# Four cross-attention layers on one core: two scaled tiles of a narrow layer added into one, entries in one plan with a new list

## The chip, the cores and the metric
One core of one Trainium2 chip runs the whole program. The metric is the device time in microseconds, as the median of runs. Engines: PE (TensorE), DVE (VectorE), ACT (ScalarE), POOL (GpSimd) and SP (SyncE, which only issues DMAs here).

## The reference
The stream x has 4 batches of 1024 tokens with 256 channels, the context 4 x 154 x 512. Layers 0 and 2 are wide (16 heads of 64, a mask on two pairs of keys), layers 1 and 3 narrow (RMS norm first, 16 heads of 16 that share 4 key-value groups). All add to the stream.

```python
# wide                                   # narrow
q, k, v = x @ Wq, ctx @ Wk, ctx @ Wv     # xn = x * rsqrt(mean(x*x) + eps) * norm_w
logits = q.k * 64**-0.5 + col_bias       # q, k, v = xn @ wq, ctx @ wk, ctx @ wv
out = softmax(logits) @ v                # out = softmax(q.k * 16**-0.5) @ v   (k, v: 4 groups)
x = x + out @ Wo + bo                    # x = x + out @ wo
```

## The kernel before
The program has three parts: prepare (weights split into a high and a low float32 part, keys and values of all layers made and stored in DRAM), run_layers, and store_outputs. The change is in run_layers, with small edits in prepare.

**Tiles.** Work is done transposed, channels on partitions and 512 tokens along the free axis. A batch is two token halves; a wide and a narrow layer on both halves make four chunks: 0 wide half 0, 1 narrow half 1 (of the batch before), 2 wide half 1, 3 narrow half 0. Each chunk has four steps, so a window has 16 steps, four heads each. There are 8 windows (4 batches, 2 pairs of layers), and the ones at either end are only partly filled.

**A step.** The list ORDER is a text of entries; every engine walks it in the same order and does its own part of each entry. query makes q on PE (L1271), ACT and DVE split it into q_pair and q_aux (L1033 to L1034, L1170 to L1173). max is a bf16 product of one (narrow) or two (wide) passes (L1290, L1286) into one of three PSUM banks called general, reduced by DVE to row maxima (L1183). turn transposes the maxima. rest and score are the products (L1314 to L1317, L1325 to L1326) into two banks, ACT takes the exponential (L1046). value multiplies by v into out_ps (L1341 to L1367), and ACT copies to the buffer kept (L1068), 12 tiles of 128 x 512.

**After a chunk.** sums: SP stores the softmax sums to DRAM and loads them spread over the partitions. inverse: DVE takes reciprocals (L1190), SP stores them (L934) and broadcasts those of the first pair of tiles into inv_b (L906, spread_inverses: 2 DMAs if wide, 4 if narrow). scale n k: POOL multiplies two tiles of kept by inv_b (L1143), then SP broadcasts the next pair. norm: ACT copies both tiles to a_hi (L1082). low: DVE makes a_lo = kept - a_hi (L1196). output: PE multiplies by the output weights (L1384) for both halves of the channels, tile by tile, with three passes for a split product (hi hi, hi lo, lo hi), and DVE adds to x (L1216). A wide chunk has four such batches of two tiles, a narrow chunk two: OUT_BATCHES = (4, 2, 4, 2).

**Narrow tiles.** A narrow tile holds one key-value group's four heads in four blocks of 32 partitions. In each block 16 rows are the head's output and the other 16 hold the sum, since the value matrix has 16 columns of v and 16 of ones; the weights no have zeros in the rows of the sums. Two groups that follow each other have their blocks exchanged in pairs (block_of).

**Keys and weights.** nkeys n (four parts, 13 DMAs each, 14 in the first) and wkeys n load the next keys through SP's queue (L847, L815), in the places that the list gives them. At window 4 the second pair of layers begins: SP also loads the other query, output and narrow weights (L769, L792, L805), behind the entries that free them.

**Order around the change.** An entry with "-" belongs to the window before, with "+" to the one after. The bank of a use of general is its number among such uses in the list modulo 3, and bank() (L1239) makes PE wait for the reader of the use three before that is present. Engines are in order: whatever an entry waits for holds everything behind it on that engine.

## Time and profile before

| | us |
|---|---|
| median of 3 runs | 1891.38 (1888.63 to 1896.26) |
| profiled execution | 1886.37 |
| its span | 1883.9 |
| PE busy | 1703.7 (90%) |
| DVE busy | 1251.6 (66%) |
| ACT busy | 1040.1 (55%) |
| POOL busy | 428.8 (23%) |

A name such as general<-a_hi,wo_hi says what an instruction writes and reads. PE's passes overlap: one is shown as busy until its last row is out, though the next has begun. In brackets behind a row of a timeline stands the engine's idle time before it and what ended it.

### The profile page before, as it was taken

The numbers are of one execution on the slowest core, as the hardware profiler recorded it, in microseconds if no ns is written. First come the engines' busy times: TensorE is split into PE (matmuls) and PEld (weight loads), VectorE is DVE, ScalarE is ACT, GpSimd is POOL, SyncE is SP. The second block draws the span as 40 slices with busy tenths as digits, with TensorE's granted clock in tenths as the row PEclk, the third lists the DMA queues.
The fourth block names the chain that finished last, engine by engine and source line by source line (L and its number), as shares of the span: only waits on it lengthen the run. The fifth ranks groups of instructions, "written<-read, shape, count | busy, mean of one in ns | idle before, by whom it ended". The sixth has DMA issues, their size and how long they took to land. (4 is left out here: it accounts for less than half of the span.)

```text
span 1883.9 us, 29965 instructions
## 1 busy us (share of the span) xinstructions
PE 1703.7 (90%) x10924; PEld 935.7 (50%) x10924; DVE 1251.6 (66%) x2393; ACT 1040.1 (55%) x1761; POOL 428.8 (23%) x299
## 2 busy tenths in 40 slices
PE   6897597989999999999899999899999999999574
PEld 5786333444545454545445454445454545454333
DVE  4447554667867786878566777577777777776342
ACT  1111063666666666666566666566666666666231
POOL 4242302121222122212111322121212121312201
PEclk9998698999999999999999999999999999999786
DMA  8976542051215121513243324222332233221205
GB/s 270 326 266 207 130 125 47 13 102 35 75 44 124 35 75 44 124 36 95 69 100 76 88 49 101 58 70 60 83 65 71 60 82 66 70 60 50 56 25 201
DMA packets 176025, 175.78 MB, mean 93 GB/s; under 512 B 89538, under 2 KB 131902, under 8 KB 174281
## 3 DMA queue, kind: packets, MB, share of 16 engines
q1 hardware_dynamic: 173576, 163.39, 33.0%
q10 hardware_dynamic: 2304, 10.49, 1.4%
q8 instruction: 88, 1.44, 0.3%
q14 instruction: 57, 0.46, 0.1%
HBM read 127.17 MB, written 46.63 MB: 92 GB/s over the span
## 5 line engine op out<-in xcount | busy, mean ns | idle before, releaser
L1183 DVE TENSOR_REDUCE tops<-general 128x2 bf16<-128x308 f32 x1024 | 436.6, 472 | 105.3 <-PE general L1290 47.8
L1143 POOL TENSOR_TENSOR kept<-kept,inv_b 128x512 f32<-128x512 f32 x192 | 258.6, 1368 | 659.6 <-DMA inv_b<-scratch_inverses 655.3
L1046 ACT ACTIVATE probs<-score_ps 128x512 f32<-128x512 f32 x512 | 299.4, 597 | 137.9 <-PE score_ps L1326 130.4
L1170 DVE CAST q_aux<-q_pair 64x512 bf16<-64x512 f32 x160 | 82.7, 517 | 211.4 <-ACT q_pair L1034 210.3
L1056 ACT ACTIVATE q_aux<-general 4x512 bf16<-4x512 bf16 x320 | 187.6, 586 | 13.6 <-PE general L1297 6.7
L1033 ACT ACTIVATE q_pair<-general 64x512 fp32r<-64x512 f32 x160 | 94.6, 592 | 178.3 <-PE general L1271 178.0
L1082 ACT ACTIVATE a_hi<-kept 128x512 fp32r<-128x512 f32 x192 | 109.9, 621 | 122.3 <-POOL kept L1143 62.8
L1196 DVE TENSOR_TENSOR a_lo<-kept,a_hi 128x512 fp32r<-128x512 f32 x192 | 149.8, 821 | 28.6 <-ACT a_hi L1082 27.8
L1216 DVE TENSOR_TENSOR x<-general,x 128x512 f32<-128x512 f32 x160 | 108.4, 690 | 80.5 <-PE general L1384 79.2
L1286 PE MATMUL general<-w_top,q_aux 128*128 128x154 bf16 x1024 | 125.7, 234 | 24.0 <-DVE q_pair L1173 10.5
L1131 POOL TENSOR_TENSOR x_lo<-xn,x_hi 128x1024 fp32r<-128x1024 f32 x32 | 75.8, 2368 | 308.0 <-ACT x_hi L1014 157.1
L1341 PE MATMUL out_ps<-probs,w_val 128*64 128x512 f32 x512 | 136.5, 617 | 0.7 <-ACT probs L1046 0.7
L1290 PE MATMUL general<-n_top,q_aux 128*128 128x308 bf16 x512 | 129.5, 301 | 6.7 <-DVE q_aux L1171 2.9
L1068 ACT ACTIVATE kept<-out_ps 128x512 f32<-128x512 f32 x192 | 104.2, 595 | 56.5 <-PE sum_ps L1355 41.5
L1325 PE MATMUL score_ps<-q_pair,n_pair 128*128 128x512 f32 x256 | 124.3, 494 | 8.6 <-ACT probs L1046 7.1
L1271 PE MATMUL general<-x_hi,wq_hi 128*128 128x512 f32 x256 | 114.8, 449 | 19.0 <-POOL x_lo L1131 18.6
L1286 PEld LDWEIGHTS general<-w_top,q_aux 128*128 128x128 bf16 x1024 | 79.0, 99 | 103.2 <-issue 38.0
L1384 PE MATMUL general<-a_hi,wo_hi 128*128 128x512 f32 x256 | 112.4, 439 | 14.8 <-DVE q_pair L1173 6.6
L1325 PE MATMUL score_ps<-q_pair,w_pair 128*128 128x512 f32 x256 | 122.1, 481 | 0.8
L1172 DVE TENSOR_TENSOR q_pair<-general,q_pair 64x512 fp32r<-64x512 f32 x160 | 109.5, 684 | 5.0
L1173 DVE TENSOR_TENSOR q_pair<-general,q_pair 64x512 fp32r<-64x512 f32 x160 | 111.0, 694 | 2.2
L1046 ACT ACTIVATE probs_rest<-score_ps 128x512 f32<-128x512 f32 x128 | 76.3, 596 | 56.7 <-PE score_ps L1326 38.6
(150 smaller groups left out, 3249.3 us busy)
## 6 DMA issues: line engine op xcount, KB each, us to landing
inv_b<-scratch_inverses SPq DMA_DIRECT2D x128, 256.0 KB
inv_b<-scratch_inverses SPq DMA_DIRECT2D x128, 128.0 KB
xn<-scratch_stream SPq DMA_DIRECT2D x16, 512.0 KB, 3.8
w_pair<-scratch_wk_hi SPq DMA_DIRECT2D x32, 256.0 KB
x<-scratch_stream SPq DMA_DIRECT2D x16, 512.0 KB, 3.3
scratch_stream<-x SPq DMA_DIRECT2D x16, 512.0 KB, 4.0
scratch_wk_hi<-p_kout_hi SPq DMA_DIRECT2D x16, 308.0 KB
p_raw<-in_L_xattn_Wk_dram SPq DMA_DIRECT2D x4, 1024.0 KB, 6.9
```

The source lines that it names most:

```text
L1046: nc.scalar.activation(dst, score_ps[:, number % 2, :], ACT.Exp, scale=scale).then_inc(act_exp.sem, 1)
L1056: last = nc.scalar.activation(q_aux[a:a + 4, half_of(n), slot(n), j, :], ps[0:4].bitcast(BF16)[:, 0:TOK], ACT.Copy, scale=-1.0)
L1143: last = nc.gpsimd.tensor_tensor(tile, tile, inv_b[:, i, :], ALU.mult)
L1173: last = nc.vector.tensor_tensor(q_pair[0:64, s, j + 1, :], ps[64:P], q_pair[64:P, s, j + 1, :], ALU.subtract)
L1183: last = nc.vector.tensor_reduce(tops[:, n % 2, sub, 2 * pair:2 * pair + 2], src, AX_X, ALU.max)
L1196: last = nc.vector.tensor_tensor(a_lo[:, i, :], kept[:, place(tile), :], a_hi[:, i, :], ALU.subtract)
L1271: last = nc.tensor.matmul(ps, l, r, start=(i == 0), stop=(i == len(pairs) - 1))
L1286: last = nc.tensor.matmul(ps[:, i * KEYS:(i + 1) * KEYS], q[:, 2 * pair + i, sub], w_top[:, 4 * (n % 4) + 2 * pair + i, :], start=True, st ...
L1290: last = nc.tensor.matmul(ps[:, 0:2 * KEYS], q[:, n % 2, sub], n_top[:, h:h + 2, :].rearrange("p h k -> p (h k)"), start=True, stop=True)
L1325: nc.tensor.matmul(ps, keys[0], q_pair[:, s, unit, :], start=True, stop=False)
L1341: last = nc.tensor.matmul(out_ps[64 * i:64 * i + 64, k, :], w_val[:, h * DW:(h + 1) * DW], probs[:, 2 * k + i, :], start=True, stop=False, ...
L1384: last = nc.tensor.matmul(ps, l, r, start=(i == 0), stop=(i == len(pairs) - 1))
```

## The change
In a narrow batch, the inverses are spread into a buffer of their own, inv_n, which is zero in the rows of the other group's place, so that scaling also clears the rows of the sums. For this, prepare puts v of every second group in the other 16 columns of a block. POOL then adds the second tile to the first (with a wait for its own product). norm, low and output handle that one tile, and the weights no hold both groups in one tile of 128 rows. The inverses in DRAM are doubled, one for wide and one for narrow chunks; an inverse therefore waits for the chunk two before. The rows of the sums are stored with two DMAs. inv_n takes 8 DMAs of 16 rows each, where 4 of 32 rows and two tiles were.

Beside that, the entries of all windows are written out once into one PLAN, with those left out that don't exist. Banks of general and score_ps follow from the number in this plan. ORDER is a new list with the same entries in another order (one max entry, one norm and one low are in the window beside).

```diff
-        sums=d("sums", (H, TOK), F32), inverses=d("inverses", (H, TOK), F32),
+        sums=d("sums", (H, TOK), F32), inverses=d("inverses", (2, H, TOK), F32),
...
-                    last = nc.vector.tensor_copy(nvout[0:m, n % OUTS, :, 0:DN], ps[0:m, bank, 0:KVN * DN].rearrange("p (g d) -> p g d", g=KVN))
+                    src = ps[0:m, bank, 0:KVN * DN].rearrange("p (v g d) -> p v g d", g=2, d=DN)
+                    dst = nvout[0:m, n % OUTS].rearrange("p (v g) d -> p v g d", g=2)
+                    for g in range(2):
+                        last = nc.vector.tensor_copy(dst[:, :, g, g * DN:g * DN + DN], src[:, :, g, :])
...
-            nc.gpsimd.memset(nvout[:], 0.0).then_inc(s_pool, 1)
-            pool.wait_ge(s_pool, 2)
-            for u in range(KVN):
-                nc.gpsimd.memset(nvout[:, :, u, DN:], 1.0)
+            nc.gpsimd.memset(nvout[:], 1.0)
...
 ORDER = """
...
-    rest 8, output 0 1, score 8 0, max 9 0, max 9 1, score 8 1, max 9 2, score 8 2, max 9 3, norm 0 2,
-        max 9 4, value 8 0, max 9 5, nkeys 0 0, max 9 6, max 9 7, score 8 3, scale 0 3, low 0 2, sums 1,
-        query 10 0, turn 9, inverse 1, value 8 1, output 0 2, max 10 0, norm 0 3, low 0 3, nkeys 0 1,
-    rest 9, max 10 1, max 10 2, query 10 1, score 9 0, score 9 1, output 0 3, squares 3, score 9 2,
-        max 10 3, score 9 3, max 10 4, value 9 0, max 10 5, max 10 6, square 3, max 10 7, query 11 0,
-        query 11 1, turn 10, value 9 1, rate 3, max 11 0, max 11 1,
-    rest 10, max 11 2, score 10 0, max 11 3, nkeys 0 2, max 11 4, max 11 5, score 10 1, nkeys 0 3,
-        max 11 6, max 11 7, score 10 2, score 10 3, query 12 0, turn 11, scale 1 0, early 0+, value 10 0,
-        value 10 1, max 12 0, max 12 1, max 12 2,
...
-    rest 13, max 14 7, score 13 0, max 15 0, max 15 1, score 13 1, max 15 2, score 13 2, turn 14,
-        score 13 3, low 1 1, wkeys 0+ 1, max 15 3, query 0+ 0, scale 2 0,
-    rest 14, output 1 1, norm 2 0, value 13 1, max 15 4, max 15 5, score 14 0, max 15 6, scale 2 1,
-        score 14 1, max 15 7, max 0+ 0, max 0+ 1, score 14 2, max 0+ 2, low 2 0, score 14 3, max 0+ 3,
-        turn 15, query 0+ 1,
-    rest 15, value 14 1, score 15 0, output 2 0, wkeys 0+ 2, score 15 1, max 0+ 4, wkeys 0+ 3, score 15 2,
-        norm 2 1, max 0+ 5, max 0+ 6, score 15 3, max 0+ 7, low 2 1, query 1+ 0, turn 0+, value 15 1,
-        scale 2 2, output 2 1, norm 2 2, scale 2 3, max 1+ 0, low 2 2, query 1+ 1
...
+    rest 1, score 1 0, output 2- 3, score 1 1, max 2 1, squares 1, score 1 2, max 2 2, max 2 3, value 1 0,
+        max 2 4, max 2 5, square 1, sums 3-, score 1 3, max 2 6, max 2 7, query 3 0, query 3 1, turn 2,
+        value 1 1, rate 1, max 3 0,
+    rest 2, inverse 3-, max 3 1, max 3 2, max 3 3, early 2, score 2 0, max 3 4, score 2 1, scale 3- 0,
+        max 3 5, max 3 6, score 2 2, max 3 7, score 2 3, query 4 0, turn 3, value 2 0, value 2 1, max 4 0,
+        max 4 1, max 4 2,
+    rest 3, max 4 3, max 4 4, max 4 5, score 3 0, max 4 6, score 3 1, max 4 7, max 5 0, norm 3- 0,
+        score 3 2, max 5 1, score 3 3, low 3- 0, max 5 2, query 6 0, turn 4, scale 3- 1, value 3 0,
+        max 5 3, value 3 1, max 5 4, sums 0, max 5 5, max 5 6,
...
+    rest 8, low 0 1, max 9 2, max 9 3, query 9 1, score 8 0, sums 1, score 8 1, output 0 1, norm 0 2,
+        value 8 0, max 9 4, score 8 2, max 9 5, max 9 6, score 8 3, max 9 7, nkeys 0 0, low 0 2,
+        query 10 0, nkeys 0 1, turn 9, nkeys 0 2, value 8 1, output 0 2, max 10 0, norm 0 3, low 0 3,
+        query 10 1,
+    rest 9, score 9 0, output 0 3, score 9 1, max 10 1, max 10 2, squares 3, score 9 2, nkeys 0 3,
+        max 10 3, value 9 0, max 10 4, max 10 5, square 3, score 9 3, max 10 6, max 10 7, query 11 0,
+        query 11 1, turn 10, value 9 1, rate 3, inverse 1, max 11 0, max 11 1,
+    rest 10, max 11 2, max 11 3, score 10 0, max 11 4, score 10 1, max 11 5, max 11 6, score 10 2,
+        max 11 7, score 10 3, query 12 0, value 10 0, turn 11, scale 1 0, value 10 1, max 12 0, max 12 1,
+        max 12 2,
+    rest 11, max 12 3, score 11 0, max 12 4, max 12 5, score 11 1, max 12 6, max 12 7, score 11 2,
+        max 13 0, score 11 3, max 13 1, max 13 2, norm 1 0, value 11 0, max 13 3, early 0+, low 1 0,
+        max 13 4, query 14 0, turn 12, value 11 1, max 13 5, sums 2, scale 1 1,
+    rest 12, wkeys 0+ 0, max 13 6, max 13 7, max 14 0, score 12 0, output 1 0, turn 13, score 12 1,
+        max 14 1, score 12 2, max 14 2, max 14 3, max 14 4, score 12 3, norm 1 1, max 14 5, max 14 6,
+    rest 13, inverse 2, value 12 1, low 1 1, split 0+, max 14 7, score 13 0, max 15 0, max 15 1,
+        score 13 1, output 1 1, scale 2 0, wkeys 0+ 1, turn 14, score 13 2, score 13 3, max 15 2, max 15 3,
+        query 0+ 0, wkeys 0+ 2,
+    rest 14, value 13 1, max 15 4, max 15 5, wkeys 0+ 3, score 14 0, score 14 1, norm 2 0, max 15 6,
+        scale 2 1, max 15 7, scale 2 2, max 0+ 0, score 14 2, max 0+ 1, turn 15, low 2 0, score 14 3,
+        scale 2 3, max 0+ 2, query 0+ 1,
+    rest 15, output 2 0, value 14 1, score 15 0, max 0+ 3, score 15 1, max 0+ 4, max 0+ 5, norm 2 1,
+        score 15 2, score 15 3, max 0+ 6, max 0+ 7, low 2 1, query 1+ 0, turn 0+, query 1+ 1, value 15 1,
+        output 2 1
 """
...
+def plan():
+
+    entries = []
+    for r in range(-1, ITER + 1):
+        entries += [(r + turn, what, n, k) for what, n, k, turn in WINDOW if present(r + turn, what, n)]
+    return entries
+
+
+PLAN = plan()
...
-GENERAL = [(*x, m) for x in WINDOW if x[0] in ("query", "max", "turn", "output", "square", "rate")
-           for m in range(KC if x[0] == "output" else 1)]
-assert len(GENERAL) % GB == 0
-BANK = {(*use[:3], use[4]): i % GB for i, use in enumerate(GENERAL)}
+GENERAL = [(*x, m) for x in PLAN if x[1] in ("query", "max", "turn", "output", "square", "rate")
+           for m in range(KC if x[1] == "output" else 1)]
+USE = {use: i for i, use in enumerate(GENERAL)}
...
-        no = [sb(f"no_{a}", [P, KVN, C], F32R) for a in ("hi", "lo")]
+        no = [sb(f"no_{a}", [P, KVN // 2, C], F32R) for a in ("hi", "lo")]
...
-        inv_b = sb("inv_b", [P, 2, TOK])
+        inv_b, inv_n = sb("inv_b", [P, 2, TOK]), sb("inv_n", [P, 2, TOK])
...
-        sums_stored, sums_loaded = signal("sums_stored", "sums", times=16), signal("sums_loaded", "sums", times=16)
-        inv_stored, inv_loaded = signal("inv_stored", "inverse", times=16), signal("inv_loaded", "scale", times=64)
+        sums_stored, sums_loaded = signal("sums_stored", "sums", times=32), signal("sums_loaded", "sums", times=16)
+        inv_stored = signal("inv_stored", "inverse", times=16)
+        inv_loaded = [Signal(sem("wide_inv_loaded"), ("scale",), 32, (0, 2)), Signal(sem("narrow_inv_loaded"), ("scale",), 16 * 8, (1, 3))]
...
+        pool_parts = Signal(sem("pool_parts"), ("scale",), only=(1, 3))
...
-                            at = 32 * block_of(v, j)
-                            dst = no[i][at:at + DN].rearrange("p (k v) n -> p k v n", v=2)
-                            sp.dma_start(dst[:, :, v, :].bitcast(F32), src[v, j]).then_inc(narrow_out_loaded, 16)
+                            at = 32 * block_of(v, j) + DN * v
+                            sp.dma_start(no[i][at:at + DN].bitcast(F32), src[v, j]).then_inc(narrow_out_loaded, 16)
...
             def spread_inverses(c, batch):
 
-                for h in range(2 if c % 2 == 0 else 4):
+                rows = dr["inverses"][c % 2]
+                for h in range(2):
                     if c % 2 == 0:
                         dst = inv_b[64 * h:64 * h + 64, :, :]
-                        src = dr["inverses"].rearrange("(h i g) n -> g h i n", h=2, i=2)[batch:batch + 1, 1 - h]
+                        src = rows.rearrange("(h i g) n -> g h i n", h=2, i=2)[batch:batch + 1, 1 - h]
+                        sp.dma_start(dst, src.to_broadcast([64, 2, TOK])).then_inc(inv_loaded[0].sem, 16)
                     else:
-                        dst = inv_b[32 * h:32 * h + 32, :, :]
-                        src = dr["inverses"].rearrange("(j g) n -> j g n", g=4)[h:h + 1, 2 * batch:2 * batch + 2]
-                    sp.dma_start(dst, src.to_broadcast([dst.shape[0], 2, TOK])).then_inc(inv_loaded.sem, 32 if c % 2 == 0 else 16)
-
-            def one_round(r):
-
-                for what, c, k, turn in WINDOW:
-                    w = r + turn
-                    if not present(w, what, c):
-                        continue
+                        for j in range(4):
+                            at = 32 * j + DN * h
+                            src = rows[4 * j + 2 * batch + h:4 * j + 2 * batch + h + 1]
+                            sp.dma_start(inv_n[at:at + DN, h, :], src.to_broadcast([DN, TOK])).then_inc(inv_loaded[1].sem, 16)
...
-                            sp.dma_start(dr["sums"], wide_sums[0:P:8]).then_inc(sums_stored.sem, 16)
+                            sp.dma_start(dr["sums"], wide_sums[0:P:8]).then_inc(sums_stored.sem, 32)
                         else:
                             wait(sp, act_keep.sem, act_keep.after(w, "value", 4 * c + 3, 1))
                             at = place(chunk_tile(c, 0))
-                            sp.dma_start(dr["sums"].rearrange("(j g) n -> j g n", g=4),
-                                         kept[DN:P:32, at:at + 4, :]).then_inc(sums_stored.sem, 16)
+                            for v in range(2):
+                                sp.dma_start(dr["sums"].rearrange("(j g v) n -> j g v n", g=2, v=2)[:, :, v, :],
+                                             kept[DN * (1 - v):P:32, at + v:at + 4:2, :]).then_inc(sums_stored.sem, 16)
                         before_w, before = back_chunk(w, c)
                         wait(sp, dve_invert.sem, dve_invert.after(before_w, "inverse", before, 0))
                         wait(sp, sums_stored.sem, sums_stored.after(w, what, c, 0))
...
                     elif what == "inverse":
 
                         wait(sp, dve_invert.sem, dve_invert.after(w, what, c, 0))
-                        before_w, before = back_chunk(w, c)
+                        before_w, before = (w, c - 2) if c > 1 else (w - 1, c + 2)
                         wait(sp, pool_scale.sem, pool_scale.after(before_w, "scale", before, OUT_BATCHES[before] - 1))
-                        sp.dma_start(by_part(dr["inverses"]), inv[:]).then_inc(inv_stored.sem, 16)
+                        sp.dma_start(by_part(dr["inverses"][c % 2]), inv[:]).then_inc(inv_stored.sem, 16)
...
-                    for i in range(2):
+                    for i in range(1 + (n + 1) % 2):
                         tile = chunk_tile(n, 2 * k + i)
                         last = nc.scalar.activation(a_hi[:, i, :], kept[:, place(tile), :], ACT.Copy)
                     last.then_inc(act_norm.sem, 1)
...
-                    wait(pool, inv_loaded.sem, inv_loaded.after(it, what, n, k))
+                    wait(pool, inv_loaded[n % 2].sem, inv_loaded[n % 2].after(it, what, n, k))
                     wait(pool, act_keep.sem, act_keep.after(it, *tile_key(chunk_tile(n, 2 * k + 1))))
+                    tiles = [kept[:, place(chunk_tile(n, 2 * k + i)), :] for i in range(2)]
                     for i in range(2):
-                        tile = kept[:, place(chunk_tile(n, 2 * k + i)), :]
-                        last = nc.gpsimd.tensor_tensor(tile, tile, inv_b[:, i, :], ALU.mult)
+                        last = nc.gpsimd.tensor_tensor(tiles[i], tiles[i], (inv_b, inv_n)[n % 2][:, i, :], ALU.mult)
+                    if n % 2:
+                        last.then_inc(pool_parts.sem, 1)
+                        wait(pool, pool_parts.sem, pool_parts.after(it, "scale", n, k))
+                        last = nc.gpsimd.tensor_tensor(tiles[0], tiles[0], tiles[1], ALU.add)
                     last.then_inc(pool_scale.sem, 1)
 
...
                     wait(dve, act_norm.sem, act_norm.after(it, "norm", n, k))
-                    for i in range(2):
+                    for i in range(1 + (n + 1) % 2):
                         tile = chunk_tile(n, 2 * k + i)
                         last = nc.vector.tensor_tensor(a_lo[:, i, :], kept[:, place(tile), :], a_hi[:, i, :], ALU.subtract)
                     last.then_inc(dve_low.sem, 1)
...
-            def bank(it, use):
-
-                at = [(*g[:3], g[4]) for g in GENERAL].index(use)
-                turn, back = GENERAL[at][3], at - GB
-                while True:
-                    what, n, k, of, m = GENERAL[back % len(GENERAL)]
-                    w = it - turn + of + back // len(GENERAL)
-                    if present(w, what, n):
-                        break
-                    if back < -3 * len(GENERAL):
-                        return general[:, BANK[use], :]
-                    back -= GB
-                read = reader[what]
-                wait(pe, read.sem, read.after(w, what, n, k) - (read.times - 1 - m if what == "output" else 0))
-                return general[:, BANK[use], :]
+            def bank(use):
+
+                if USE[use] >= GB:
+                    w, what, n, k, m = GENERAL[USE[use] - GB]
+                    read = reader[what]
+                    wait(pe, read.sem, read.after(w, what, n, k) - (read.times - 1 - m if what == "output" else 0))
+                return general[:, USE[use] % GB, :]
...
-                        pairs = [q for i in range(2) for q in split3(w[0][:, 2 * k + i, rows], w[1][:, 2 * k + i, rows], a_hi[:, i, :], a_lo[:, i, :])]
+                        tiles = [(2 * k + i, i) for i in range(2)] if n % 2 == 0 else [(k, 0)]
+                        pairs = [q for at, i in tiles for q in split3(w[0][:, at, rows], w[1][:, at, rows], a_hi[:, i, :], a_lo[:, i, :])]
```

## Rows read from the trace of the kernel before

**Rows 1.** Page, head and part 1: busy us (share), instructions, of each engine.
```profile
span 1883.9 us, 29965 instructions
...
PE 1703.7 (90%) x10924; PEld 935.7 (50%) x10924; DVE 1251.6 (66%) x2393; ACT 1040.1 (55%) x1761; POOL 428.8 (23%) x299
```

**Rows 2.** Windows: length, busy (count) of each engine, clock, DMA share, GB/s.
```profile
core 0: us, PE busy (x) PEld busy (x) DVE busy (x) ACT busy (x) POOL busy (x), PEclk, DMA share, GB/s
...
1141.80:1339.00 197.20, 187.00 (x1250) 95.97 (x1248) 139.12 (x266) 125.39 (x216) 42.98 (x30) 0.98 0.29 69
1339.00:1527.40 188.40, 186.06 (x1250) 95.74 (x1248) 141.00 (x266) 125.55 (x217) 43.98 (x30) 1.00 0.31 70
```

**Rows 3.** Timeline of ACT: start, length, what; the x_hi splits of the same step.
```profile
1339.04 1.06 ACT L1014 ACTIVATE x_hi<-xn 128x1024 fp32r<-128x1024 f32 x1
...
1527.42 1.06 ACT L1014 ACTIVATE x_hi<-xn 128x1024 fp32r<-128x1024 f32 x1
```

**Rows 4.** Groups of PE by line and shape: busy, mean ns, idle before.
```profile
L1384 PE MATMUL general<-a_hi,no_hi 128*128 128x512 f32 x128 | 56.7, 443 | 20.7 <-DVE a_lo L1196 19.4 <-DVE q_pair L1173 1.3
```

**Rows 5.** Timeline of PE: output passes in a row.
```profile
471.54 0.40 PE L1384 MATMUL general<-a_lo,no_hi 128*128 128x512 f32 x1
...
473.87 0.39 PE L1384 MATMUL general<-a_hi,no_lo 128*128 128x512 f32 x1
```

**Rows 6.** Timeline of PE: four short bf16 passes, then a float32 one.
```profile
924.66 0.43 PE L1286 MATMUL general<-w_top,q_aux 128*128 128x154 bf16 x4
924.89 0.47 PE L1325 MATMUL score_ps<-q_pair,w_pair 128*128 128x512 f32 x1
925.21 0.39 PE L1326 MATMUL score_ps<-q_aux,w_aux 128*128 128x512 bf16 x1
```

**Rows 7.** Timeline of PE: what follows the large holes; idle time in brackets.
```profile
932.65 0.79 PE L1271 MATMUL general<-x_hi,nq_hi 128*128 128x512 f32 x1 [6.42 <-DMA n_val_rest<-scratch_nv_rest]
...
975.66 0.49 PE L1325 MATMUL score_ps<-q_pair,n_pair 128*128 128x512 f32 x1 [3.52 <-ACT probs L1046]
...
1192.92 1.94 PE L1314 MATMUL score_ps<-q_pair,w_rest 128*32 128x512 f32 x8 [9.19 <-issue]
```

**Rows 8.** Timeline of SP, the DMA queue: start, length, what is issued.
```profile
917.93 0.60 SPq L847 DMA_DIRECT2D n_pair<-scratch_nk_hi  x1
...
930.79 0.40 SPq L847 DMA_DIRECT2D n_val_rest<-scratch_nv_rest  x1
931.23 1.73 SPq L906 DMA_DIRECT2D inv_b<-scratch_inverses  x4
...
1169.22 5.05 SPq L805 DMA_DIRECT2D no_hi<-scratch_no_hi  x8
1174.31 5.52 SPq L805 DMA_DIRECT2D no_lo<-scratch_no_lo  x8
...
1190.25 1.30 SPq L906 DMA_DIRECT2D inv_b<-scratch_inverses  x2
```

**Rows 9.** Waits: engine, line, for whom; us in total, times, longest.
```profile
ACT a_hi L1082 <- POOL kept L1143: 62.8, 14, 12.8
```

**Rows 10.** Timeline of the tail: SP, POOL, PE.
```profile
1833.35 8.44 SPq L906 DMA_DIRECT2D inv_b<-scratch_inverses  x8
...
1837.59 2.48 POOL L1143 TENSOR_TENSOR kept<-kept,inv_b 128x512 f32<-128x512 f32 x2 [45.74 <-DMA inv_b<-scratch_inverses]
...
1842.63 0.79 PE L1384 MATMUL general<-a_hi,no_hi 128*128 128x512 f32 x1 [16.48 <-DVE a_lo L1196]
...
1847.49 0.53 PE L1384 MATMUL general<-a_hi,no_lo 128*128 128x512 f32 x1
```

**Rows 11.** Page, part 5, three groups; last, a line: ns min/median/max.
```profile
L1143 POOL TENSOR_TENSOR kept<-kept,inv_b 128x512 f32<-128x512 f32 x192 | 258.6, 1368 | 659.6 <-DMA inv_b<-scratch_inverses 655.3
...
L1082 ACT ACTIVATE a_hi<-kept 128x512 fp32r<-128x512 f32 x192 | 109.9, 621 | 122.3 <-POOL kept L1143 62.8
...
L1196 DVE TENSOR_TENSOR a_lo<-kept,a_hi 128x512 fp32r<-128x512 f32 x192 | 149.8, 821 | 28.6 <-ACT a_hi L1082 27.8
...
L1170 DVE CAST q_aux<-q_pair x160: 408/420/1502, 222.3 to 1796.3; 64x512 bf16<-64x512 f32 x160
```

110 lines of the change are left out of this document (46 added, 64 removed).

## The prediction
> **What bounds the kernel now.** I read first the page's part on each engine: PE is busy for 1703.7 of 1883.9 us, DVE for 1251.6 [rows 1]. That is an average over stages, so the next view is one period of the schedule. Its length is the distance between two x_hi splits of the same step: 1339.04 to 1527.42, 188.4 us [rows 3]. In that window PE is busy for 186.06 us at full granted clock, DVE for 141.00, ACT for 125.55, POOL for 43.98 [rows 2]: PE leaves 2.3 us free, the next engine 47. The window before it has the same work and is 8.8 us longer [rows 2]; its hole comes below. A busy PE may still be slow, since a pass is shown longer than it holds the engine, so I look at starts: eleven output passes in a row start between 471.54 and 473.87, ten distances in 2.33 us, though each is shown 0.39 to 0.40 long [rows 5]. I call these 0.233 us a slot. Slots stand back to back in the steady windows; what is taken off PE there is taken off the window, as long as the producers keep up. Third, PE's large holes, places that only the order decides: 6.42 us before 932.65, waiting for narrow keys, 3.52 us for ACT before 975.66, 9.19 us before 1192.92 [rows 7].
>
> **Passes removed.** A narrow batch made 2 output halves x 2 tiles x 3 split products = 12 passes, now 2 x 1 x 3 = 6. There are 16 narrow half layers of two batches each, so 32 x 6 = 192 passes go, half of three groups of 128 (one is shown) [rows 4]. At 0.233 us: 44.7 us. The most it can be is the group's shown mean, 0.443 us, 85 us [rows 4], which counts the overlap of passes twice, so I stay with the slot; the least is what the producers let through, rival B. A pass itself stays as it is: the same 512 columns, the same 128 rows, of which all now carry data.
>
> **Work moved to and from the others.** ACT loses 32 copies to a_hi of 0.621 us, 19.9 us, and DVE 32 subtractions to a_lo of 0.821 us, 26.3 us [rows 11]. Neither bounds a window, so both count as nothing there: PE's stream covers them. In the tail, where that cover is gone, they are counted. POOL gains 32 additions, priced by its products of the same form, 1.37 us, 43.8 us in all [rows 11]. With 44 of 188 us in use it has room [rows 2]. The addition also waits for the second product; no row shows such a wait, and I take 0.1 us (none to 1 us).
>
> **The SP queue.** A narrow batch issues 8 broadcasts where it issued 4, and 4 took 1.73 us [rows 8]: 1.7 us more. With POOL's addition a narrow batch is ready 3.1 us later. Behind these issues stand the early load and the next batch's spread. The chain: 4.24 us from the first issue to POOL's start (1833.35 to 1837.59) [rows 10], + 1.7, then 2 x 1.37 less overlap (shown 2.48) + 1.37 + 0.1; the store of the inverses before it I bound by what is left of the 4.24 after its issues, 2.5 us. Together 12.4 us from the reciprocal to an added tile. A step is 188.4 / 16 = 11.8 us. In the new list norm 3- 0 stands about 1.6 steps, 19 us, behind inverse 3-, and norm 1 0 as far behind inverse 1. So some 6 us of room are left, and ACT does not wait. The new wait of an inverse, for the chunk two before instead of one, is weaker than the old one: nothing.
>
> **POOL against DVE.** A cast to q_aux takes 0.408 us at least, 0.420 in the middle and 1.502 at most [rows 11]; I take the longest to lie beside POOL's work. If each of the 32 additions met one, DVE would lose 32 x 1.08 = 35 us; if none, nothing. POOL works in under a quarter of a window and DVE has 47 us of room: I take 1 us. The Trainium skill (SBUF — State Buffer, Who interferes with whom) says that GpSimd locks out, for its whole instruction, a DVE copy in a two-port mode or a DVE instruction with two SBUF inputs. By that rule, the spread of the cast's times agrees.
>
> **The new list.** (a) A float32 pass behind short bf16 ones isn't ready in time: four wide max passes from 924.66, the score pass at 924.89, the next at 925.21 [rows 6], 0.32 us instead of a slot, 0.09 more (part of it, down to none, may be given back by the last max). The new list has 42 switches from a wide max to such a pass, the old 36: 6 x 0.09 x 8 = +4.1 us. (b) The hole before 932.65. SP issued the last two key parts from 917.93 to 930.79 [rows 8], 6.5 us each, one step behind their entries. In the new list inverse 1 stands behind all four parts, and the first three follow each other without a wait from the end of step 7: 26 us, over before step 10's query 12 with some 10 us to spare: -6.4 us. (c) The hole before 1192.92. SP issued 16 pieces of the narrow output weights in 10.6 us (1169.22 to 1179.83), then an inverse's spread and two parts of the wide keys until 1190.25 [rows 8]. The 16 pieces remain; output 1 1 stands 0.6 steps earlier (-7 us), but three parts instead of two are behind it (+4.6): -2 us. (d) The hole before 975.66 is an inverse that came late behind rows of keys; now the rows go first: -1.5 us (0 to -3.5). (e) Whether the new list opens small gaps of its own, the old trace can't show. The nearest row is PE's idle time in a window, 2.3 us [rows 2]; I take no difference, and 2 us a window either way, 16 in all, for the range.
>
> **Both ends.** Preparation makes 8 more DVE copies of 64 columns; the nearest row, 0.821 us for 512 [rows 11], bounds them at 6.6 us, and I take 1. In the tail each step waits for the one before. The sums take one issue more, +0.5; the first batch comes 3.1 later for spread and addition, 0.6 and 0.7 earlier for ACT's and DVE's second tile; POOL's second start is 1.7 + 1.4 later again. But the old second batch had waited until twelve passes were over, at 0.44 us each (1842.63 to 1847.49 for eleven) [rows 10]; now there are six, and six more after. Followed through, DVE's last addition ends 2 us later than before: +2 us.
>
> **Sum.** -44.7 + 4.1 - 6.4 - 2 - 1.5 + 1 + 1 + 2 = -46.5 us. The profiled execution took 1886.37 us (2.5 us outside its span): 1839.9. It lies 5.0 us below the median of 1891.38, which is what will be compared: 1844.9 us.
>
> **Rivals.**
> A. As above, PE's slots bound every window: 1844.9, own range 1827 to 1861 from (e). 0.72.
> B. DVE sets the pace locally: the max passes use three banks that DVE empties, and the output passes were the time in which it caught up. Then only what DVE itself lost counts, 26.3 instead of 44.7 us: 1863. For it: DVE is busy for 141 of 188 us. Against: PE is idle for 2.3 us of a window. 0.10.
> C. Slower. The 6 us of room between inverse and norm aren't there, because SP still issues keys; then each of the 32 narrow batches holds ACT, in whose queue the exponentials stand behind the norm, for the chain's 3.1 us, 99 us: 1944. It decides where the chain of 12.4 us is longer than the list's distance. For it: ACT has waited for POOL 14 times, 62.8 us in all [rows 9]. Against: the distances counted above. 0.06.
> D. POOL's additions meet a cast each time, and each cast stands ahead of max passes: +34: 1879. 0.04.
> E. The list closes small gaps too, 2 us a window: 1829 or below. 0.08.
> That no passes are removed is excluded by the loops.
>
> **How the numbers follow.** The prediction is A's, 1844.9. A, B and E's larger part make up the range of 1825 to 1869; C, D and the lower part of E are left out. A measurement of this kernel can tell about 0.5%, 9.5 us, from no change. Faster by more: A, B, D and E, less 0.05 for mishaps that add up: 0.89. Within: 0.04. Slower: C and 0.01 of those: 0.07.
>
> **What would show it.** Right: 192 passes on the narrow output weights; a window of 182 to 184 us with PE idle for as little; no hole before query 12 in the fourth window, one of 5 to 9 us at the wide rest of the sixth; the tail 2 us longer. Wrong: a window of 185 to 188 us with PE waiting for tops (B), a_hi waiting for POOL in each narrow batch (C), casts with a mean far above 0.52 us (D), new holes before outputs or values (e).

## Result and the profile after

The changed kernel took 1842.7 us (median of four runs, 1835.02 to 1844.97), the kernel before 1890.14 us beside it. The ratio is 0.9738, with a 95% interval of 0.9717 to 0.9759: 49 us, or 2.6%, faster. The prediction was 1844.9 us. The profiled execution took 1840.65 us, where the sum had ended at 1839.9.

The head and first part of the page of the changed kernel, to be read beside [rows 1]:

```profile
span 1838.9 us, 29698 instructions
...
PE 1658.9 (90%) x10732; PEld 898.9 (49%) x10732; DVE 1226.8 (67%) x2370; ACT 1023.5 (56%) x1729; POOL 462.2 (25%) x327
```

PE has exactly 192 instructions fewer (10924 before), ACT 32 fewer, POOL 28 more (32 additions, and fewer of other kinds). PE's busy time fell by 44.8 us, the span by 45.0, and PE's share stayed at 90%. The three groups of output passes on the narrow weights count 64 each instead of 128 [rows 4]. The kernels differ in length, so the same line of the program has another number in each (the narrow output passes stand at L1384 before, at L1389 in the change, at L1385 to L1390 in the kernels below). Groups of PE, POOL and ACT, columns as there:

```profile
L1389 PE MATMUL general<-a_hi,no_hi 128*128 128x512 f32 x64 | 31.9, 498 | 23.8 <-DVE a_lo L1208 23.8
...
L1155 POOL TENSOR_TENSOR kept<-kept 128x512 f32<-128x512 f32 x32 | 41.5, 1298 | 2.5
...
L1090 ACT ACTIVATE a_hi<-kept 128x512 fp32r<-128x512 f32 x160 | 93.6, 624 | 103.1 <-PE general L1389 41.3 <-POOL kept L1151 33.4 <-POOL kept L1155 28.2
```

The mean of a shown pass rose from 443 to 498 ns although a pass is what it was. Half of this group's passes are the first of an output entry now, a quarter before, and a first pass is shown longer (0.50 us and more, where the others have 0.39 to 0.40). That is one more reason to count starts and not shown durations.

Two periods of the schedule, cut at the same x_hi split as [rows 2, 3]; the columns are those of [rows 2]:

```profile
1120.50:1308.80 188.30, 181.44 (x1232) 91.33 (x1224) 136.75 (x263) 123.47 (x213) 47.63 (x34) 0.99 0.30 66
1308.80:1493.40 184.60, 180.15 (x1232) 91.02 (x1224) 139.87 (x263) 123.54 (x213) 48.80 (x34) 1.00 0.30 66
```

The undisturbed period went from 188.40 to 184.60 us, the one with the hole from 197.20 to 188.30. But PE's idle time in the undisturbed one rose, from 2.3 to 4.5 us. Some of PE's waits on DVE in the whole kernel (engine, line, for whom; us in total, times, longest):

```profile
PE general L1290 <- DVE q_pair L1185: 16.9, 23, 2.2
PE general L1294 <- DVE q_pair L1185: 16.5, 13, 4.0
PE general L1294 <- DVE tops L1195: 2.4, 13, 0.2
```

L1290 and L1294 are the wide and the narrow max passes. They wait for a general bank from which DVE still reads a query (the subtraction, L1185). Before the change, PE waited for that subtraction 20.8 us in all, now 35.0 (a third line, before output passes, has 1.6).

All periods, from the same split, which readers can repeat from a timeline of ACT (us; the change is the mean of three profiled executions, whose spans are 1838.9, 1841.3 and 1840.3):

```
period               1      2      3      4      5      6   last   from last split to end
before           188.9  188.4  197.8  192.9  197.3  188.4  249.1  107.4
change           183.4  187.7  187.3  185.5  187.7  185.2  236.2  108.9
```

The stretch ahead of the first of them grew from 373.7 to 378.3 us, because the new list puts this split later; the last period gives that back, so the two belong together. The second period stands out: it moved by only 0.7 us, the first and the sixth by 5.5 and 3.2.

### The profile page after: what moved, and what is told of

It is laid out like the page before. It is cut to its first block and busy times, and to the rows that moved or that the text cites. A ratio compares the mean times of both kernels' runs of the same rounds, so it can differ in the third digit from the quotient of the medians.

```text
span 1838.9 us, 29698 instructions
## 1 busy us (share of the span) xinstructions
PE 1658.9 (90%) x10732; PEld 898.9 (49%) x10732; DVE 1226.8 (67%) x2370; ACT 1023.5 (56%) x1729; POOL 462.2 (25%) x327
## 5 line engine op out<-in xcount | busy, mean ns | idle before, releaser
L1151 POOL TENSOR_TENSOR kept<-kept,inv_b 128x512 f32<-128x512 f32 x128 | 167.0, 1326 | 427.3 <-DMA inv_b<-scratch_inverses 427.3
L1290 PE MATMUL general<-w_top,q_aux 128*128 128x154 bf16 x1024 | 130.9, 234 | 27.7 <-DVE q_pair L1185 16.9
L1090 ACT ACTIVATE a_hi<-kept 128x512 fp32r<-128x512 f32 x160 | 93.6, 624 | 103.1 <-PE general L1389 41.3
L1208 DVE TENSOR_TENSOR a_lo<-kept,a_hi 128x512 fp32r<-128x512 f32 x160 | 121.7, 793 | 39.4 <-ACT a_hi L1090 38.8
L1294 PE MATMUL general<-n_top,q_aux 128*128 128x308 bf16 x512 | 124.5, 302 | 23.5 <-DVE q_pair L1185 16.5
L1290 PEld LDWEIGHTS general<-w_top,q_aux 128*128 128x128 bf16 x1024 | 79.3, 99 | 120.4 <-issue 63.0
L1151 POOL TENSOR_TENSOR kept<-kept,inv_n 128x512 f32<-128x512 f32 x64 | 83.6, 1327 | 193.6 <-DMA inv_n<-scratch_inverses 193.6
L1389 PE MATMUL general<-a_hi,wo_hi 128*128 128x512 f32 x256 | 112.3, 439 | 10.0 <-DVE a_lo L1208 8.0
L1185 DVE TENSOR_TENSOR q_pair<-general,q_pair 64x512 fp32r<-64x512 f32 x160 | 110.9, 693 | 2.2
```

What stands on the lines that cost most here:

```text
L1151: last = nc.gpsimd.tensor_tensor(tiles[i], tiles[i], (inv_b, inv_n)[n % 2][:, i, :], ALU.mult)
L1185: last = nc.vector.tensor_tensor(q_pair[0:64, s, j + 1, :], ps[64:P], q_pair[64:P, s, j + 1, :], ALU.subtract)
L1208: last = nc.vector.tensor_tensor(a_lo[:, i, :], kept[:, place(tile), :], a_hi[:, i, :], ALU.subtract)
L1290: last = nc.tensor.matmul(ps[:, i * KEYS:(i + 1) * KEYS], q[:, 2 * pair + i, sub], w_top[:, 4 * (n % 4) + 2 * pair + i, :], start=True, st ...
L1294: last = nc.tensor.matmul(ps[:, 0:2 * KEYS], q[:, n % 2, sub], n_top[:, h:h + 2, :].rearrange("p h k -> p (h k)"), start=True, stop=True)
L1389: last = nc.tensor.matmul(ps, l, r, start=(i == 0), stop=(i == len(pairs) - 1))
```

## Experiments

Twelve more runs were made: nine other kernels, one of them twice, and the change itself twice more. Two theories stood at the start. **Theory 1** is the sum of the prediction: PE's slots bound the window, a removed pass is worth its slot of 0.233 us, wherever it stands. **Theory 2** is rival B in a sharper form: passes are also the time in which DVE, ACT and POOL finish what PE needs next, so what a removed pass is worth depends on what the list puts behind it. Periods and spans below are of the profiled executions, ratios are to the kernel before, with 95% intervals.

**The old list with the new arithmetic.** All of the change, but with the entries in their old order:

```diff
- ORDER = (the new entries)
+ ORDER = (the entries of the kernel before)
```

> The changed kernel with the list of before: the added tile, the halved passes and the plan stay, the order goes back. Theory 1 (every pass removed is a slot of PE removed; the new list itself is worth little): a window of 188.4 - 5.6 = 182.8 us and about 1850 us in all, since the holes of before at the narrow and wide keys (6.4, 3.5 and 9.2 us) come back. Theory 2 (the old list has no room for the longer chain of a narrow batch: 12.4 us against about 13 from inverse 3- to norm 3- 0): a_hi waits for POOL twice in each window and the window stays at 186 or more, 1870 us or more.

Measured: ratio 0.9980 [0.9963, 0.9997], 1886.5 us. 192 passes are gone and almost nothing came of it, in the steady stretch either: its first, second and sixth period take 188.1, 187.0 and 188.7 us, where the kernel before has 188.9, 188.4 and 188.4.

**The new list with the old arithmetic.** The kernel before, with only its list replaced:

```diff
- ORDER = (the entries of the kernel before)
+ ORDER = (the new entries)
```

> The kernel before with the new list alone: two tiles and twelve passes per narrow batch. Theory 1 (the small gaps of 1.2 to 2 us that the changed kernel shows twice in a window before a narrow max pass belong to the new list, which puts a max onto a bank that DVE still reads for a query): the same gaps here, a window near 189 us, and with the holes at the keys gone 1885 us. Theory 2 (the gaps come from POOL's additions and are none of the list's): no such gaps, a window of 188 or less, 1878 us or less.

Measured: ratio 0.9949 [0.9927, 0.9971], 1882.9 us, so 9.6 us come from the list alone. Its periods are 187.6, 188.8, 189.6, 193.6, 197.1 and 191.4 us: the third lost its 8 us hole, the fifth is as long as before, and the quiet ones (first, second, sixth) are longer by 0.7 us on average. The fifth has another hole than before, though. The 9.19 us ahead of the wide rest are gone; 4.90 us stand ahead of a value instead (timeline of SP, then PE):

```profile
1152.42 5.04 SPq L808 DMA_DIRECT2D no_hi<-scratch_no_hi  x8
1157.50 5.03 SPq L808 DMA_DIRECT2D no_lo<-scratch_no_lo  x8
...
1173.65 1.93 PE L1364 MATMUL out_ps<-probs,n_val 128*32 128x512 f32 x8 [4.90 <-ACT probs L1049]
```

**Twelve passes in the new list.** The change with each narrow output's products issued twice; the second time starts the sum anew, so the result is unchanged:

```diff
-                        for i, (l, r) in enumerate(pairs):
-                            last = nc.tensor.matmul(ps, l, r, start=(i == 0), stop=(i == len(pairs) - 1))
+                        for again in range(1 + n % 2):
+                            for i, (l, r) in enumerate(pairs):
+                                last = nc.tensor.matmul(ps, l, r, start=(i == 0), stop=(i == len(pairs) - 1))
```

> The changed kernel with the six passes of each narrow batch made twice into the same bank, the second time from its start, so that PE has the work of before and all else is as changed. If PE's slots bound every window: 192 x 0.233 = 44.7 us more than the changed kernel, 1887. If DVE's pace bounds where the passes were taken out: only part of it, 20 us or less, 1863.

Measured: ratio 0.9922 [0.9896, 0.9948], span 1880.4. Against the change itself, 0.9734 in the runs below, the 192 passes cost 1.88%, 35.5 us; by the spans of the profiled executions 1880.4 - 1840.2 = 40.2 us (this profiled execution was the slowest of its four). In the new list a pass is worth 0.18 to 0.21 us, close to a slot; the intervals of the two ratios leave 0.15 to 0.22.

**Twelve passes in the old list.** The same edit on the first experiment:

```diff
- ORDER = (the new entries)
+ ORDER = (the entries of the kernel before)
...
+                        for again in range(1 + n % 2):
```

> The changed kernel with the old list of entries and with each narrow output's six matrix products issued twice, so that TensorE has the same number of passes as before the change (the result is doubled by nothing, since the second run starts its sum anew). What is new against the kernel before is only SP's own tiles, POOL's addition and the fourth reciprocal tile. Theory 1 (in the old list the removed passes were cover for DVE's, ACT's and POOL's work beside them): with the passes back the waits of old_list go too, and the time is that of the kernel before, ratio 0.998 to 1.004. Theory 2 (the waits of old_list come from the longer chain through SP's tiles and POOL's addition): the waits stay and the passes come on top, about 43 us over old_list's 1886, ratio about 1.02.

Measured: ratio 1.0015 [1.0002, 1.0028], 1892.2 us. So the time of the old list is all but the same with six passes and with twelve: the first theory of this expectation, which is theory 2 above. The four together, and what six passes less are worth in each row (the intervals leave 0.2 points either way in the first row, 0.4 in the second):

```
               twelve passes   six passes   difference
old list              1.0015       0.9980    0.35% =  6.6 us
new list              0.9922       0.9734    1.88% = 35.5 us
```

The traces show the mechanism at one place. In the old list a narrow output stands between a query and the next narrow max. With six passes (timeline of PE and DVE; start, length, engine, line, what; idle time in brackets):

```profile
1449.83 2.70 POOL L1148 TENSOR_TENSOR kept<-kept,inv_b 128x512 f32<-128x512 f32 x2 [8.56 <-DMA inv_b<-scratch_inverses]
...
1451.39 1.42 DVE L1180 CAST q_aux<-q_pair 64x512 bf16<-64x512 f32 x1
1451.47 0.50 PE L1386 MATMUL general<-a_hi,no_hi 128*128 128x512 f32 x1
...
1452.74 0.40 PE L1386 MATMUL general<-a_hi,no_lo 128*128 128x512 f32 x1
...
1453.54 0.69 DVE L1182 TENSOR_TENSOR q_pair<-general,q_pair 64x512 fp32r<-64x512 f32 x1
...
1454.29 0.30 PE L1291 MATMUL general<-n_top,q_aux 128*128 128x308 bf16 x1 [1.15 <-DVE q_pair L1182]
```

And with twelve, at the same step of the same list:

```profile
1455.35 0.50 PE L1387 MATMUL general<-a_hi,no_hi 128*128 128x512 f32 x1
1455.37 1.42 DVE L1180 CAST q_aux<-q_pair 64x512 bf16<-64x512 f32 x1
...
1457.52 0.69 DVE L1182 TENSOR_TENSOR q_pair<-general,q_pair 64x512 fp32r<-64x512 f32 x1
...
1458.03 0.40 PE L1387 MATMUL general<-a_hi,no_lo 128*128 128x512 f32 x1
...
1458.27 0.31 PE L1291 MATMUL general<-n_top,q_aux 128*128 128x308 bf16 x1
```

DVE needs the same 2.84 us in both, from the start of its second cast to the end of its last subtraction. The cast takes 1.42 us beside POOL's product, 0.42 in the middle of all; by an estimate from these two, 1.0 of DVE's 2.84 us is this lengthening, so the place is an extreme one. From the first output pass to the max it is 2.82 us with six passes, 1.15 of it idle, and 2.92 with twelve. Six passes, 1.4 us of slots, bought 0.10 us. The twelve end just as DVE does, and so no idle time is shown there. The trace of the kernel before already had the sign: at the same step its twelve passes begin at 1451.46, and the max behind them waits for the same subtraction:

```profile
1454.72 0.30 PE L1290 MATMUL general<-n_top,q_aux 128*128 128x308 bf16 x1 [0.19 <-DVE q_pair L1173]
```

Over the whole kernel (waits, columns as above), old list with six passes, then with twelve:

```profile
PE general L1386 <- DVE q_pair L1182: 12.3, 12, 2.2
PE general L1291 <- DVE q_pair L1182: 9.6, 9, 1.8
PE general L1287 <- DVE q_pair L1182: 8.5, 13, 1.0
```

```profile
PE general L1287 <- DVE q_pair L1182: 8.3, 13, 1.0
PE general L1387 <- DVE q_pair L1182: 7.5, 7, 1.7
PE general L1291 <- DVE q_pair L1182: 1.3, 3, 0.7
```

All of PE's waits on DVE and ACT, by the same view, sum to 95.5 us with twelve passes in the old list and to 126.6 with six. These 31.1 us are most of the 38 that are missing between the 44.7 of slots and the 6.6 measured. In the new list there is no such trade: with twelve passes PE waits 106.4 us for DVE and 7.5 for ACT, in the three traces of the change 99.3 to 105.0 and 9.0 to 13.4.

A second kind of such place: a score pass that waits for a bank of ACT's exponentials, while ACT stands at a_hi and waits for POOL. In the old list with six passes:

```profile
1547.55 1.15 ACT L1087 ACTIVATE a_hi<-kept 128x512 fp32r<-128x512 f32 x2 [4.01 <-POOL kept L1148]
...
1550.20 0.49 PE L1326 MATMUL score_ps<-q_pair,n_pair 128*128 128x512 f32 x1 [2.13 <-ACT probs L1051]
```

With twelve passes the a_hi at 1551.44 waits 2.51 us, and the score pass that answers, at 1554.33, for nothing. So the two waits are not a cost of the new tiles or of POOL's addition alone, which old_list_twelve has too: they come when the passes go. In the new list that output (output 3- 1, line 533 before, line 535 after) stands between two scores, and the three others beside scores and turns; there the passes are worth most of their slots. That these places make the difference is argued from the list and the sums of waits; no run moved a single entry.

**What the addition costs.** The change without POOL's addition and the wait ahead of it (the second group's part is then missing from the result of the narrow layers):

```diff
-                    if n % 2:
-                        last.then_inc(pool_parts.sem, 1)
-                        wait(pool, pool_parts.sem, pool_parts.after(it, "scale", n, k))
-                        last = nc.gpsimd.tensor_tensor(tiles[0], tiles[0], tiles[1], ALU.add)
```

> The changed kernel without POOL's addition (and the wait before it), so that the output misses the second group. If the addition is hidden, as the prediction had it: 1 to 2 us less in the tail and no more, 1840. If POOL's additions hold DVE's casts at places where PE waits: the two gaps per window shrink and 5 to 10 us go, 1835.

Measured: ratio 0.9671 [0.9640, 0.9703], 1828.8 us: 0.6%, 12 us, below the change. That was not expected, so it was run again, with the change and a kernel with one addition too many beside it:

> The changed kernel without POOL's addition and the wait ahead of it; the second group's part is missing from the output of the narrow layers. If the addition of 1.3 us lies beside other work but for the tail, as the prediction said, the ratio is that of the change on the same chip less 1 to 3 us (0.972 to 0.973). If it costs what the first such run showed, the ratio is 0.967, some 12 us below the change.

```diff
+        spare, spare_ready = sb("spare", [P, 3, TOK]), sem("spare_ready")
...
                     last.then_inc(pool_scale.sem, 1)
+                    if n % 2:
+                        nc.gpsimd.tensor_tensor(spare[:, 2, :], spare[:, 0, :], spare[:, 1, :], ALU.add)
```

> The changed kernel with one more addition of POOL for each narrow batch and quarter (32 in all, 1.3 us each), on tiles that nobody else uses, behind the step's last signal. It lengthens no chain but POOL's own, and blocks DVE's and ACT's use of SBUF as the real one does, if it does. Theory 1 (the addition costs little where it stands): within 3 us of the change. Theory 2 (each addition delays DVE's casts, and these reach TensorE): 5 to 13 us above the change, as leaving one out would save.

> The changed kernel itself, beside the three others on the same chip, as what they are compared with: ratio 0.9735 as in the two looks before, between 0.971 and 0.976.

Measured: without the addition 0.9669 [0.9647, 0.9692]; with two 0.9748 [0.9729, 0.9768]; the change 0.9730 [0.9707, 0.9753]. The addition costs about 0.6%, 12 us, by the medians, and 7.4 us between the mean spans of the profiled executions (1840.2 in three of the change and the one with two additions, 1832.8 in two without; both of these were the slowest of their runs, so the medians are the better measure). A second addition that nobody waits for adds 0.2%, less than the intervals can tell from nothing. The steady period is the same with one, none and two (the change is shown above; here without the addition, then with two):

```profile
1307.10:1491.80 184.70, 179.56 (x1218) 90.97 (x1224) 140.21 (x263) 123.56 (x214) 43.56 (x30) 1.00 0.29 65
```

```profile
1307.00:1491.60 184.60, 179.10 (x1217) 91.04 (x1224) 138.94 (x263) 123.56 (x213) 53.77 (x38) 1.00 0.29 66
```

POOL is busy for 43.56, 48.80 and 53.77 us in the three, and the length doesn't move: in the steady stretch neither POOL's time nor what it blocks on DVE reaches PE. Part of the cost is in the tail, where two batches' additions stand one behind the other on the path. The change, then the kernel without the addition:

```profile
1794.83 1.26 POOL L1155 TENSOR_TENSOR kept<-kept 128x512 f32<-128x512 f32 x1
...
1797.54 0.79 PE L1389 MATMUL general<-a_hi,no_hi 128*128 128x512 f32 x1 [17.90 <-DVE a_lo L1208]
...
1806.37 0.80 PE L1389 MATMUL general<-a_hi,no_hi 128*128 128x512 f32 x1 [5.91 <-DVE a_lo L1208]
```

```profile
1790.34 0.79 PE L1385 MATMUL general<-a_hi,no_hi 128*128 128x512 f32 x1 [16.45 <-DVE a_lo L1204]
...
1797.96 0.79 PE L1385 MATMUL general<-a_hi,no_hi 128*128 128x512 f32 x1 [4.69 <-DVE a_lo L1204]
```

That is 1.45 + 1.22 = 2.7 us. By the x_hi splits the same executions give the 7.4 us as follows: the two kernels without the addition are ahead by 0.7 us at the end of the sixth period and by 3.9 at the last split, and the stretch behind it is 3.6 us shorter (105.9 and 104.8 us, where those with it have 108.6 to 109.1). At the last split the two differ by 4.1 us from each other, so only the 3.6 stand clear of scatter. Where the rest of the 12 us of the medians lies is not shown.

**The narrow output weights.** One trace of the change has a hole of 3.98 us in what the prediction calls the sixth window. Timeline of SP, POOL, ACT and PE there:

```profile
1130.08 3.67 SPq L813 DMA_DIRECT2D no_hi<-scratch_no_hi  x8
...
1133.79 4.68 SPq L813 DMA_DIRECT2D no_lo<-scratch_no_lo  x8
...
1138.52 1.23 SPq L912 DMA_DIRECT2D inv_b<-scratch_inverses  x2
...
1144.81 2.50 POOL L1151 TENSOR_TENSOR kept<-kept,inv_b 128x512 f32<-128x512 f32 x2 [13.47 <-DMA inv_b<-scratch_inverses]
...
1147.35 1.15 ACT L1090 ACTIVATE a_hi<-kept 128x512 fp32r<-128x512 f32 x2 [6.22 <-POOL kept L1151]
1148.40 1.06 ACT L1054 ACTIVATE probs<-score_ps 128x512 f32<-128x512 f32 x2
...
1149.52 1.93 PE L1365 MATMUL out_ps<-probs,n_val 128*32 128x512 f32 x8 [3.98 <-ACT probs L1054]
```

Sixteen pieces take SP's queue for 8.4 us; the inverses' spread stands behind them, POOL starts on it 6.3 us after its issue, and POOL, ACT's queue and PE wait one after the other. It is the hole of the new list alone, smaller. Four kernels were run on this and on the waits for q_pair. First the change itself again:

> The changed kernel once more, as the mark for the three beside it, whose differences are under one per cent: a ratio to the kernel before of 0.974, within its interval of 0.972 to 0.976.

Measured: 0.9734 [0.9708, 0.9760], and this trace has no hole there; its largest near it is 1.91 us at 1134.37. Nor has the third trace of the change. In both the sixteen pieces took 7.4 us. Then the pieces behind the last part of the wide keys:

```diff
-                        if w == B:
-                            wait(sp, pe_output.sem, pe_output.after(w, what, c, k))
-                            load_narrow_out(1)
...
                         load_wide_keys(p, b, k)
+                        if (w, k) == (B + 1, 3):
+                            wait(sp, pe_output.sem, pe_output.after(B, "output", 1, 1))
+                            load_narrow_out(1)
```

> The changed kernel with the 16 pieces of the second pair's narrow output weights issued behind the wide keys instead of ahead of them. If the hole of 4.4 us in the sixth window and the slow clock behind it come from SP's order: 5 to 7 us less than the changed kernel. If the other loads of that place (keys, values) are late by themselves: 2 us or less.

Measured: 0.9751 [0.9730, 0.9772]: no gain, and none of the 5 to 7 us of its first theory. Since the hole stands in one of three traces of the change, its mean cost is a third of that or so, which this run can't tell from nothing. Then DVE's two subtractions, which free the query's bank, ahead of its two casts:

```diff
+                    nc.vector.tensor_tensor(q_pair[64:P, s, j, :], ps[0:64], q_pair[0:64, s, j, :], ALU.subtract)
+                    last = nc.vector.tensor_tensor(q_pair[0:64, s, j + 1, :], ps[64:P], q_pair[64:P, s, j + 1, :], ALU.subtract)
+                    last.then_inc(dve_query.sem, 1)
                     nc.vector.tensor_copy(q_aux[0:64, t, s, j, :], q_pair[0:64, s, j, :])
                     nc.vector.tensor_copy(q_aux[64:P, t, s, j + 1, :], q_pair[64:P, s, j + 1, :]).then_inc(dve_aux.sem, 1)
```

> The changed kernel with DVE's four instructions of a query in another order: the two subtractions that read the PSUM bank ahead of the two casts, so that the bank is free 0.84 us sooner, and over 1.8 us where POOL holds a cast. If the gaps before narrow max passes are waits for that bank: they shrink by half or more, 1.5 to 2.5 us a window, 12 to 20 us in all. If the casts themselves are what is late (the max of the next step reads q_aux): nothing is gained or some us are lost.

> Both of these edits together. They touch different waits, so the sum of the two: 17 to 25 us less than the changed kernel by the theory of the bank, 5 to 7 by the other.

Measured: 0.9729 [0.9706, 0.9752] for the order of DVE, 0.9737 [0.9714, 0.9759] for both; 12 to 20 and 17 to 25 us had been expected of the theory of the bank. The waits for the subtraction did go, from 35.0 to 4.2 us in all, and others grew in their place (waits of the kernel with the subtractions first):

```profile
PE general L1294 <- DVE tops L1195: 13.5, 16, 1.6
PE general L1290 <- DVE tops L1195: 7.7, 16, 2.5
PE general L1294 <- DVE q_pair L1183: 1.8, 1, 1.8
```

PE's waits for the maxima (tops) rose from 4.9 to 23.2 us in all and those for the casts (q_aux) from 5.4 to 12.7; together with the subtraction 45.3 before the reordering and 40.1 after. All of PE's waits on DVE, whatever the tile, sum to 99.3 us here and to 99.3, 103.0 and 105.0 in the three traces of the change. What is late at such a place is DVE's work as a whole, more than the one instruction that the trace names. None of these versions beats the change by more than the intervals.

## Why the prediction was right, point by point

**Passes removed, -44.7 us.** Right in kind in the new list, where the runs give 35 to 40 us, 4.5 to 9 less than the 44.7. The step that priced a removed pass at its slot "as long as the producers keep up" held there for most passes. It said nothing on the order, and in the old list it fails almost wholly: 6.6 us. Rival B, which had 0.10, describes the old list with six passes in its mechanism; what it had as its price (only DVE's own 26.3 us would count) was still too much for that list.

**Idle time as evidence against rival B.** The prediction held against B that PE is idle for only 2.3 us of a window [rows 2]. That shows that PE was bound with the passes in place; it can't say how long the producers would have kept it waiting without them. At 1458 us above, with twelve passes, DVE's last subtraction ends at 1458.21 and the max starts at 1458.27: no idle time, and yet nothing to be gained by fewer passes.

**Window of 182 to 184 us with PE idle for as little.** Measured 184.6 in the profiled execution and 185.2 in the mean of three, idle 4.5 us instead of 2.3. The three quiet periods (first, second, sixth) sum to 556.3 us instead of 565.7, -3.1 each where -5.1 was forecast (-5.6 for passes, +0.5 for switches). The step that failed is (e), the list's own small gaps, taken as nothing; the 2 us a window of its range was the size it has. With the new list alone the quiet periods grew by 0.7 us, and PE's wait for the subtraction rose from 20.8 to 39.3 us in the whole kernel, so the list brings such gaps without the new arithmetic. One of them in the change:

```profile
1299.00 1.33 POOL L1155 TENSOR_TENSOR kept<-kept 128x512 f32<-128x512 f32 x1
1299.21 1.41 DVE L1183 CAST q_aux<-q_pair 64x512 bf16<-64x512 f32 x1
...
1301.35 0.69 DVE L1185 TENSOR_TENSOR q_pair<-general,q_pair 64x512 fp32r<-64x512 f32 x1
...
1302.10 0.43 PE L1294 MATMUL general<-n_top,q_aux 128*128 128x308 bf16 x2 [0.73 <-DVE q_pair L1185]
```

**The holes, -9.9 us for (b) to (d).** They gave more. Before, the third, fourth and fifth period exceeded the mean quiet one of 188.6 by 22.3 us together; now they exceed the mean quiet one of 185.4 by 4.2. So 18.1 us closed. (b) is right as told: in the changed kernel the last part of the narrow keys is issued by 909.1 us, ahead of the inverse at 910.70, PE doesn't wait at query 12, and this hole closes with the list alone, too (-8.2 us in the third period). (c) was wrong in its place and its size: there is no hole of 5 to 9 us before the wide rest. That one is gone with the list alone, and the pieces move the wait to a value: 4.90 us with the list alone, where they took 10.1 us, 3.98 in one of three traces of the change, where they took 8.4, and at most 0.4 in the two others (7.4 us) and in the kernel with twelve passes in the new list (7.9 us; its fifth period is 193.6, the list alone has 197.1). So it doesn't take the missing passes to close it; the shorter issue of the smaller pieces fits all five traces, but was not tried by itself. (d) was not followed up: the fourth period is 193.6 us with the list alone, 195.0 with twelve passes beside, and 185.5 in the change, and what took the 7.4 us off stays open.

**The SP queue and rival C.** The chain from inverse to norm was to fit with 6 us of room, and ACT's waits don't speak against it: a_hi waited for POOL 61.6 us in 18 waits, before 62.8 in 14 [rows 9]; for an addition only in 4, 28.2 us, of which 15.3 are one wait of the tail. C's mechanism is real, though: it is what the trace above shows once, behind the 16 pieces.

**POOL against DVE, 1 us, and rival D.** The addition at 1299.00 meets a cast, which takes 1.41 instead of 0.42 us. That agrees with the rule of the Trainium skill that the prediction quoted (SBUF — State Buffer, Who interferes with whom). The casts as a whole got slower by little: the mean of the first of a query went from 517 to 508 ns, that of the second from 524 to 574, together 6.6 us for all 320. Without the addition the second still takes 569, so most of this isn't the addition's. And with a second addition the steady period stays at 184.6 us. D is out.

**The addition as a whole.** Underestimated: the kernel is 7 to 12 us faster without it, where the sum had 1 us for the casts and some 3 of the tail's terms. Behind the last split it is 3.6 us, near those terms; the rest is not located.

**Preparation and tail, +3 us.** From the last split to the end it was 107.4 us and is 108.9: +1.5 for a forecast of +2. The two waits before the last narrow outputs are 17.90 and 5.91 us, 4.4 more than the 16.48 [rows 10] and 2.90 of before, against six passes fewer ahead of the second. The stretch ahead of the first split and the last period changed by -8.3 us together; two windows' -10.2 and preparation's +1 make -9.2.

**Errors that cancelled.** Over six periods the small gaps cost 11.7 us more than forecast (1.9 each), and the holes gave 8.2 more. With +0.9 at the ends of the schedule, -0.5 in the tail and POOL's 1 us, which is in the periods already, the forecast of -46.5 becomes -43.6, the -43.7 of the mean spans but for rounding. The profiled execution lay 2.0 us under its median, not 5.0. That the total fits to 2 us is partly luck. That PE's slots carry most of the gain in the new list is not: the passes alone, put back, cost 35 to 40 us. But the prediction gave the list itself only its switches and holes; that the passes are worth anything only because of the new order was in no term of the sum.

## What to carry over

Ahead of removing work from the bound engine, look at each place at what that engine does next and when its producer will be done: where the removed work ends just as the producer does, the engine's idle time is near zero and the work is worth near nothing as well. Such work pays only with an order that puts something else, or nothing that waits, behind it. Here list and arithmetic had to be changed together (0.5% and 0.2% alone, 2.6% together), and a table of two by two showed it. Where a wait names one of several instructions of an engine, moving that one forward can merely move the wait to the next, as it did here with the subtraction.

## What the hardware showed that was not expected

After the hole of 3.98 us PE's granted clock fell for a while. Windows of the changed kernel (columns as in [rows 2]):

```profile
1144.00:1149.00 5.00, 1.54 (x6) 0.93 (x6) 0.47 (x1) 1.66 (x4) 2.50 (x2) 1.00 1.28 185
1149.00:1153.00 4.00, 3.48 (x25) 0.44 (x25) 3.04 (x6) 3.90 (x8) 0.00 (x0) 0.57 1.28 175
```

In the second the mean granted clock is 0.57, near the lower of its two levels, 1.2 of 2.4 GHz. Eight value passes took 1.93 us there and 1.07 at 1138.13, so, as an estimate, at 0.57 for 4 us such a hole costs 1.7 us beside its length. The sum had priced the holes of before by their idle times alone. Before, the clock was 0.50 in the 3.4 us behind the hole of 6.42 and 0.64 in the 4.1 us behind that of 9.19, and 1.00 behind that of 3.52. In the length of the third period the difference shows, 9.4 us above the sixth with an idle time of 6.42; in that of the fifth it does not, 8.9 with 9.19 [rows 7].

The three profiled executions of the change have spans within 0.2% and still differ by up to 2.2 us in single periods (the first: 182.5, 184.6 and 183.1; the second: 186.3, 188.5 and 188.3), and a hole of 4 us is there in one and not in the next. A single trace can show a mechanism; what it costs needs the runs.
